# DLRM tower on one Trainium2 core: six fields picked on TensorE instead of four, 13 gathers a block, smaller rings

## What is computed

```
e = stack([tbl_f[ids[:, f]] for f in range(32)], axis=1)      # [2048, 32, 256]
dots = einsum('bnd,bmd->bnm', e, e)
z = dots[:, iu, ju]                                           # i < j, 496 numbers
h = concatenate([z, dense_ctx], axis=1)                       # 496 + 16 = 512
h = maximum(h @ W_top1 + b_top1, 0)                           # 512 -> 512
h = maximum(h @ W_top2 + b_top2, 0)                           # 512 -> 256
y = h @ W_top3                                                # 256 -> 1
```

## Time and profile before

| | |
|---|---|
| median of 3 runs | 613.19 us (612.56 to 613.61) |
| the profiled execution: its time | 611.16 us |
| the profiled execution: its span | 609.4 us, 25960 instructions |
| PE busy | 522.0 us, 86% |
| POOL busy | 432.3 us, 71% |
| DVE and ACT busy | 275.0 us (45%) and 218.9 us (36%) |
| moved by DMA | 72.16 MB, mean 118 GB/s |
| granted TensorE clock, mean | 0.992 of 2.4 GHz |

### The profile page before, as it was taken

One profiled execution on the slowest core, in us unless ns is written; L12 is line 12 of the kernel. 1 busy time (PEld: TensorE's weight loads), 2 busy tenths in 40 slices (PEclk: granted clock), 3 DMA queues, 4 the chain that ended last, 5 costly groups with the idle time before them and its releaser, 6 DMA issues.

```text
span 609.4 us, 25960 instructions
## 1 busy us (share of the span) xinstructions
PE 522.0 (86%) x11962; PEld 463.2 (76%) x11962; DVE 275.0 (45%) x596; ACT 218.9 (36%) x423; POOL 432.3 (71%) x463
## 2 busy tenths in 40 slices
PE   1349998999999998899889897988889798899875
PEld 0235795988888897879879796977879697887654
DVE  2003844737274645556354455546254555415231
ACT  1233334343333333334323334433323433343540
POOL 6776677777777777777777777777777777777700
PEclk9999999999999999999989999999999999999997
DMA  5587543443434343434334343433434333333300
GB/s 145 192 238 228 141 135 109 113 122 107 123 110 127 109 122 108 124 111 118 115 107 124 109 126 108 121 111 108 126 108 123 107 109 110 109 107 107 107 12 3
DMA packets 26415, 72.16 MB, mean 118 GB/s; under 512 B 8426, under 2 KB 9338, under 8 KB 25680
## 3 DMA queue, kind: packets, MB, share of 16 engines
q0 software_dynamic: 21888, 59.80, 35.6%
q1 hardware_dynamic: 4420, 10.72, 5.6%
HBM read 70.48 MB, written 0.01 MB: 116 GB/s over the span
## 4 chain that ended last, share of the span: by engine, by line
PE 65%; POOL 13%; DMA 10%; issue 9%; DVE 1%; ACT 1%; SPq 0%
PE ps_l L324 15%; PE ps_turn L240 15%; POOL rows L227 13%; PE ps_gram L291 12%; DMA rows<-in_table,index 10%; PE ps_pick L269 7%; PE ps_pick L271 7%; PE ps_l L338 2%; PE ps_l L255 1%; PE ps_pick L255 1%; PE ps_l L346 1%; DVE pairs L592 1%; PE ps_turn L355 0%; PE ps_wide L355 0%; PE ps_l L355 0%
## 5 line engine op out<-in xcount | busy, mean ns | idle before, releaser
L227 POOL DMA_INDIRECT rows<-in_table,index x456 | 431.5, 946 | 145.2 <-issue 120.9
L456 ACT COPY cols<-ps_turn 128x512 f32<-128x512 f32 x221 | 128.3, 590 | 320.2 <-PE ps_turn L240 319.9
L592 DVE COPY pairs<-ps_gram 32x112 f32<-32x112 f32 (+1 forms) x480 | 180.6, 376 | 134.5 <-PE ps_gram L291 128.4
L240 PE MATMUL ps_turn<-identity,rows 128*128 128x128 f32 x912 | 147.8, 290 | 51.1 <-DMA rows<-in_table,index 50.8
L240 PEld LDWEIGHTS ps_turn<-identity,rows 128*128 128x128 f32 x912 | 103.0, 145 | 69.7 <-DMA rows<-in_table,index 47.9
L291 PE MATMUL ps_gram<-cols 128*32 128x32 f32 x7936 | 108.9, 200 | 20.9 <-issue 19.4
L291 PEld LDWEIGHTS ps_gram<-cols 128*32 128x32 f32 x7936 | 90.1, 110 | 46.3 <-issue 41.4
L580 DVE TENSOR_TENSOR one_hot<-ps_wide,row_number 125x2048 fp32r<-125x2048 f32 x28 | 63.9, 2282 | 116.0 <-ACT ps_wide L473 115.9
L269 PE MATMUL ps_pick<-one_hot,table_hi 125*128 125x256 f32 x448 | 114.8, 294 | 0.4 <-ACT stage L477 0.4
L324 PE MATMUL ps_l<-pairs,w_sb 128*128 128x128 f32 x960 | 109.9, 275 | 0.6 <-DVE score L611 0.6
L271 PE MATMUL ps_pick<-one_hot,table_lo 125*128 125x256 f32 x448 | 110.0, 283 | 0.0
(11 more groups left out here) (63 smaller groups left out, 140.0 us busy)
## 6 DMA issues: line engine op xcount, KB each, us to landing
rows<-in_table,index POOLq DMA_INDIRECT x456
pick_id<-in_pick_ids SPq DMA_DIRECT2D x14, 250.0 KB
w_sb<-in_w_t SPq DMA_DIRECT2D x1, 2048.0 KB, 23.1
cols<-in_tbl SPq DMA_DIRECT2D x2, 1000.0 KB
stage<-in_tbl SPq DMA_DIRECT2D x2, 1000.0 KB
w_sb<-in_W_top SPq DMA_DIRECT2D x1, 512.0 KB, 26.8
pairs<-in_dense_t SPq DMA_DIRECT2D x16, 8.0 KB, 2.1
scores<-score SPq DMA_DIRECT2D x16, 0.5 KB
```

The source lines that it names most:

```text
L227: pool.indirect_dma_start(out=rows[x % ROWS][:, k, :], out_offset=None, in_=table, in_offset=bass.IndirectOffsetOnAxis(ap=index[:, t, i:i ...
L240: last = pe.transpose(ps_turn[x % TURNS][:, h, SPG * k:SPG * (k + 1), :], rows[x % ROWS][:, k, h * P:(h + 1) * P], identity[:, :])
L456: act.copy(cols[t % COLS][:, :, :, FPU * u:FPU * (u + 1)], ps_turn[x % TURNS][:, :, :, :]).then_inc(cols_ready, 1)
L592: last = dve.tensor_copy(pairs[n % 2][N_FIELDS * q:N_FIELDS * (q + 1), c0:KC, TQ * j + FQ * u:TQ * j + FQ * (u + 1)] .rearrange("p c g -> ...
```

## The change

- `PICKS` is 6: two more fields of 1000 rows are picked. 26 fields are left to gather in blocks 4 to 31: six whole units (`WHOLE`) of two gathers and a seventh with one gather, 2 fields of 64 samples. A block has 13 gathers, the kernel 64 + 28 * 13 = 428. There are 42 jobs; from block 5 on each tile period has three, one in the odd block (u = 4, 5) and two in the even (u = 1, 2 and u = 4, 5), up to block 28.
- The ring `rows` has 6 units in place of 8, `cols` 2 blocks in place of 3. `raw` is gone, and the DMA descriptor scratch of a partition is set to 4096 bytes.
- `split_table` is gone from PE. ACT makes the high part as before, DVE subtracts it from the table (`make_lo`). The raw tables land in `w1_sb` and `stage`, so that the weights of layer 1 are loaded after three tables are split.
- `relu2` and `take_score` go from DVE to ACT. Gram of an odd block (done in the even one) starts at u = 0, gram of an even block is in two pieces in place of four; layer 2 is at u = 3 and layer 3 at u = 6 of an even block. In the last block `early_layer1` of the first half stands behind the last transposes.

```
-PICKS = 4
+PICKS = 6
-    ROWS, COLS, TURNS = 8, 3, 3
+    ROWS, COLS, TURNS = 6, 2, 3
+    def jobs(t):
+        if 2 <= t < SETTLED:                      # SETTLED = 5
+            return [2 * t - 4, 2 * t - 3]
+        q = 3 * ((t - SETTLED) // 2) + PICKS
+        return [] if t < 2 or q >= JOBS else [q] if t % 2 == 1 else [q + 1, q + 2]
-        return {2: (0, 4), 3: (4, 8), 4: (8, 12), 5: (12, 16)} if t % 2 == 1 else {1: (0, 6), 2: (6, 11), 3: (11, 16)}
+        return {2: (0, 8), 3: (8, 16)} if t % 2 == 1 else {0: (0, 6), 1: (6, 11), 3: (11, 16)}
...
-            sp.wait_ge(table_loaded[0], 16)
-            load_table(2)
-            sp.wait_ge(table_loaded[1], 16)
+            for j in range(2, 4):
+                sp.wait_ge(table_loaded[j - 2], 16)
+                load_table(j)
+            sp.wait_ge(lo_ready, 3)
+            load_table(4)
             sp.dma_start(w1_sb[:, :, :], w1_t).then_inc(w1_loaded, 16)
...
+                    if t >= 1 and u in gram_parts(t):
+                        gram(t - 1, *gram_parts(t)[u])
+                    if 3 <= t < BLOCKS - 1 and t % 2 == 1:
+                        if u == 1:
+                            layer1((t - 3) // 2)
+                    if 4 <= t and t % 2 == 0:
+                        if u == (0 if t == BLOCKS - 2 else 3):
+                            layer2((t - 4) // 2)
+                        if u == (2 if t == BLOCKS - 2 else 6):
+                            layer3((t - 4) // 2)
+                    if t % 2 == 0 and jobs(t):
+                        if u in (1, 2):
+                            pick(jobs(t)[0], u - 1)
+                        if u in (4, 5):
+                            pick(jobs(t)[1], u - 4)
+                    if t % 2 == 1 and jobs(t):
+                        if u in (4, 5):
+                            pick(jobs(t)[-1], u - 4)
...
                         if u == 5:
-                            early_layer1(0, M1C // 2)
+                            spin(1)
+            early_layer1(0, M1C // 2)
             half_gram(1)
...
# ACT, odd block with jobs: c is its job
+                        if u == 5:
+                            take_pick(c)
                     if t > BPG and t % BPG != 0 and u == (2 if t == BLOCKS - 1 else 5):
                         place(t)
...
# DVE
+            def make_lo(j):
+                dve.wait_ge(hi_ready, j + 1)
+                dve.tensor_tensor(table_lo[:, j, :, :], table_raw[j], table_hi[:, j, :, :].bitcast(F32),
+                                  ALU.subtract).then_inc(lo_ready, 1)
```

More of the change, by code:

```diff
@@ L61, in dlrm_tower, with gathers, landed @@
     LATE = N_FIELDS - EARLY
-    def last_gathers(v):
-        return [((2 * v + k) // UNITS, (2 * v + k) % UNITS) for k in range(SUBS)]
+    def gathers(t, u):
+        if t < BPG:
+            return [(s, u) for s in range(SUBS)]
+        if t < BLOCKS - 1:
+            return [(s, u) for s in range(SUBS)] if u < WHOLE else [(0, WHOLE)]
+        if u == UNITS // 2:
+            return [(0, WHOLE)]
+        v = u if u < UNITS // 2 else u - 1
+        return [((2 * v + k) // WHOLE, (2 * v + k) % WHOLE) for k in range(SUBS)]
+    def landed(x):
+        return 16 * sum(len(gathers(t, u)) for t in range(BLOCKS) for u in range(units(t))
+                        if unit(t, u) <= x and unit(t, u) % ROWS == x % ROWS)
+    def jobs(t):
[3 more added lines that the diff above has]
+        return [] if t < 2 or q >= JOBS else [q] if t % 2 == 1 else [q + 1, q + 2]
     def gram_parts(t):
@@ L233, in _, with transposes @@
         def _(pe):
-            def transposes(x):
-                pe.wait_ge(gathered[x % ROWS], 16 * SUBS * (x // ROWS + 1))
+            def transposes(t, u):
+                x = unit(t, u)
+                pe.wait_ge(gathered[x % ROWS], landed(x))
                 if x >= TURNS:
@@ L522, in regroup_half_upper, with relu2, take_score @@
                 moved.then_inc(half_pairs_ready, 1)
-            act.wait_ge(identity_ready, 1)
-            act.mul(minus_identity[:, :], identity[:, :], -1.0).then_inc(minus_ready, 1)
+            def relu2(n):
+                act.wait_ge(l2_done, n + 1)
+                for m in range(M2C):
+                    last = act.activation(hidden2[:, m, :], ps_late_l2[m] if n == TILES - 2 else ps_l1[:, m, :],
+                                          ACT.Relu, bias=b2_sb[:, m:m + 1])
+                last.then_inc(hidden2_ready, 1)
+            def take_score(n):
+                act.wait_ge(l3_done, n + 1)
+                if n >= 2:
+                    act.wait_ge(stored[n % 2], 16 * (n // 2))
+                act.copy(score[:, n % 2, :], ps_late_l3 if n == TILES - 2 else ps_l1[0:1, M2C, :]
+                         ).then_inc(score_ready, 1)
             spread_ids(0)
@@ L707 @@
     starts = np.cumsum([0] + [tables[f].shape[0] for f in order])[:-1].astype(np.uint32)
-    index_t = ids[:, order].reshape(blocks, BLOCK // SPG, SPG, units, FPU).transpose(2, 4, 0, 3, 1)
-    index_t = dram("index_t", index_t.reshape(P, -1).astype(np.uint32))
-    base_t = dram("base_t", np.repeat(np.tile(starts.reshape(units, FPU).T, (SPG, 1)), BLOCK // SPG, axis=1))
+    whole = ids[:, order].reshape(blocks, BLOCK // SPG, SPG, units, FPU).transpose(2, 4, 0, 3, 1).reshape(P, blocks, -1)
+    base_t = np.repeat(np.tile(starts.reshape(units, FPU).T, (SPG, 1)), BLOCK // SPG, axis=1)
+    rest = (N_FIELDS - PICKS) % FPU
+    n_whole = (N_FIELDS - PICKS) // FPU
+    late = order[FPU * n_whole:FPU * n_whole + rest]
+    column = BLOCK // SPG * n_whole
+    first = GROUP // BLOCK
+    index_t = whole.astype(np.uint32)
+    index_t[:, first:, column:] = 0
+    index_t[:, first:, column] = ids[:, late].reshape(blocks, P).T[:, first:]
+    base_t = np.stack([base_t, base_t], axis=1)
+    base_t[:, 1, column] = np.tile(starts[FPU * n_whole:FPU * n_whole + rest], BLOCK)
+    index_t = dram("index_t", index_t.reshape(P, -1))
+    base_t = dram("base_t", base_t)
     table = dram("table", np.concatenate([tables[f] for f in order]))
```

222 lines of the change are left out of this document (101 added, 121 removed).

## The result

The kernel after takes 677.49 us, the median of four runs (671.94 to 680.96), where the kernel before took 613.4: 1.1028 times as long, interval 1.0944 to 1.1113. The forecast was 637 us with a range of 612 to 652. The sign was right; the time lies 25 us above the upper end.

A forecast was written before the change was run, and what follows sets the result against it. POOL set the pace before (35.0 us a period, PE 32.4); PE was to become the bound at 36.8. Start 120 + 12 * 36.8 + end 71.9 = 633.5 us of span, 637 us as measured, 3.9% slower; range 612 to 652.

The forecast's parts named there:

- What bounds the kernel: Blocks 5 to 28: PE becomes the bound, 35.9 us a period with data ready against POOL's 32.5.
- The third pick, 4.1 us a period: PE, each tile period: a third pick adds two half picks of 2.07 us, 4.14 us.
- the 34.6 that was named as a sign: Tile periods: PE busy about 34.6 us in each, as a sign that the forecast holds.
- The wait for ACT, 1.35 us: Before an odd block's gram: PE waits 1.35 us a period for `place` and a copy, queued on ACT behind `take_pick`.
- The wait of layer 1: Layer 1 waits for `take_score` on ACT: 0.6 us in every second period, 0.3 us on average.
- The step that failed is gram: Gram on PE: five pieces instead of seven save 0.2 us a period, instructions ready after a wait 0.7 us of stalls.
- The third rival: PE's stalls come from the old order: 34.5 us a period without the ACT wait, 601 us; chance 0.12.
- The start: Before the tile periods: first layer 1 at about 75 us instead of 82.3, weights landing at 71 to 77 us.
- The second rival: Late weights and landings, short ring, larger gram pieces: first layer 1 at 85 us, periods of 37.6, 658 us; chance 0.12.
- the small descriptor scratch: POOL's gathers: 4096 bytes cost nothing, or at worst a slower POOL, hidden up to 1.41 us a gather.
- From the first to the second layer 1: Start, between the first two layer 1 steps: 44 to 45 us, second at 120 us (bounds 114 and 125).
- The end: From layer 1 of block 29 on: 71.9 us instead of 76.4 (bounds 69 and 75), first step 22.5 instead of 25.5.

The follow-up runs named there:

- Fourteen gathers: The kernel after, but POOL gathers the seventh unit of blocks 4 to 31 twice, 14 gathers a block: 680.04 us, 1.1115 of the kernel before.
- a shorter third pick: The kernel after, but odd blocks' job from block 5 on does only its first and last chunks (results not right): 648.32 us, 1.0574 of the kernel before.
- the mended order: The kernel after with odd blocks' gram at u = 1, 2, 3, even blocks' gram in four pieces, and `place` at u = 4: 630.83 us, 1.0262.
- the one piece: The kernel with all three orders undone (630.83 us), but gram of an even block in one piece of 128 matmuls at u = 2: 653.29 us, 1.0674.
- gram at u = 1: The kernel after, but gram of an odd block starts at u = 1 of the next block (pieces at u = 1, 2, 3): 663.34 us, 1.0818.
- with four pieces: Even blocks' gram in four pieces against two, both with odd blocks' gram at u = 1, 2, 3 and `place` at u = 4: 630.83 against 637.29 us.
- the first gap filled: The kernel after with six identity matmuls ahead of each odd block's gram from 5 to 27, where PE waits for ACT: 681.87 us, 1.1108.
- three groups of seven: All three orders undone, six picks only in groups 2, 4 and 6, four picks in the others: 606.83 us, 0.9899 of the kernel before.

## Why the prediction was right in its sign and wrong in its size

**What bounds the kernel: right.** PE took over from POOL. Fourteen gathers show no change, a shorter third pick takes off 2.9 us a period.

**The third pick, 4.1 us a period: right.** Three picks fill 12.0 us of a period on the timeline of after, 4.0 each. PE's busy time, 35.1 us a period at full clock, is 0.5 above the 34.6 that was named as a sign.

**The wait for ACT, 1.35 us: right in place and size** (17.1 us in the twelve periods, 1.43 each). The wait of layer 1 was forecast at 0.6 us in every second period; up to 600 us it is 3.4 us in 6, 0.57 each. The seventh, 2.2 us, lies in the end.

**The step that failed is gram.** The text took 0.2 us off for five pieces instead of seven, and then "a gram that starts after a wait should find its instructions ready; I take off 0.7 us of the 1.4 us of stalls". Both have the wrong sign. Of the 28.0 us of stalls 20.9 lie in the twelve periods: 1.7 us a period and not 0.7. In nine of the twelve a stall follows in the very gram that waited for ACT, 11.8 us in all (one is shown below, at 422.78), so a gram that starts after a wait doesn't find its instructions. The other 9.1 us lie in the gram of two pieces. And the dense runs themselves go slower: 2.06 us for 128 where two pieces of 64 take 1.5 to 2.0 in the mended order; PE's busy time is 0.5 us a period above the 34.55 of the mended kernel's clean periods. Together 1.5 us of the 1.84 by which the clean periods lie above the forecast (38.64 - 36.8; 22 us in twelve); 0.1 more is the wait for ACT, the rest small gaps. The cause is shown by the packets of instructions, by the one piece (+25 us) and by the edits that lay longer work between the pieces: the stalls fell by 12.6 us with gram at u = 1, and from 15.6 to 5.7 us with four pieces. The third rival said that the stalls belong to the order of the work, not to PE, and gave 34.5 us a period. The mended order came to 34.88 at best. So it was right that the order makes the stalls, and wrong on which order: it blamed the four pieces, and expected the new order to be the better one.

**The clock was no term of the sum.** Three periods at 0.96 took 2.3 us more each, 7 us; of the 2.3 us PE's busy time is 1.4 and the rest is longer gaps. The kernel before has one such period too, at 0.95. A stretch ahead of a fall, then the window behind it, with its granted clock of 0.66:

```profile
418.68 1.26 PE L298 MATMUL ps_gram<-cols 128*32 128x32 f32 x96 [1.43 <-ACT cols L463]
419.87 0.66 PE L263 MATMUL ps_turn<-identity,rows 128*128 128x128 f32 x4
420.46 0.38 PE L298 MATMUL ps_gram<-cols 128*32 128x32 f32 x19
422.78 0.79 PE L298 MATMUL ps_gram<-cols 128*32 128x32 f32 x61 [1.94 <-issue]
423.50 0.58 PE L276 MATMUL ps_pick<-one_hot,table_hi 125*128 125x256 f32 x1
423.88 0.42 PE L278 MATMUL ps_pick<-one_hot,table_lo 125*128 125x256 f32 x1
```

```profile
424.50:428.00 3.50, 3.50 (x23) 3.50 (x22) 0.00 (x0) 0.36 (x1) 0.12 (x1) 0.66 0.07 22
```

PE had stood 1.43 us for ACT and 1.94 us for instructions within 5.5 us, and then the picks of 256 columns follow each other every 0.21 us and not 0.12: the lower level, 1.2 GHz. What lets it fall isn't settled: with the first gap filled one period still fell, and in the period from 127.92 on PE stood for 1.42 and 1.43 us within 5.3 us and the clock stayed at 1.00.

**The start: 8 us late.** The first layer 1 was put at 75 us and began at 83.3. The step that failed is what layer 1 waits for. The sum had it wait for the gathers of unit 25 and for its weights. It waited for neither: PE's last wait for a gather ends at 63.74 us, and the 19.6 us from there to layer 1 are nearly all PE's own work, four half picks among it, with one stall of 2.21 us and a first half pick at the lower clock, 3.5 us where the next took 2.0. Before 63.74 PE was behind on landings: it was busy for 9.64 of the 27 us from 42 to 69, and the gather issued at 52.23 landed 11.46 us later, within the 4 to 12 that were named. The second rival came close to the number (85 us). Of its reasons, the late landings held PE up until 63.74 only, and the weights didn't hold it up.

The text also put the small descriptor scratch at nothing. The timeline of POOL in the start says otherwise:

```profile
37.54 2.74 POOL L249 DMA_INDIRECT rows<-in_table,index  x1 [0.30 <-issue]
40.59 2.13 POOL L249 DMA_INDIRECT rows<-in_table,index  x1 [0.30 <-issue]
```

The same happens at 45.52 (2.65 us) and 55.99 (2.47 us), and twice between 85 and 110 us. A gather else takes 0.95. In each of the fifteen runs with 4096 bytes six gathers take 1.9 to 3.0 us, all ahead of 112 us, 8 to 10 us in all. In the two runs without it, the kernel before and the same with a ring of 6, none takes over 1.3 us, although DMA was as busy in the start (254 GB/s from 33 to 42 us). That points to the scratch, but no run changes it alone. Three of the long gathers lie ahead of the one issued at 52.23, so they may have cost the start up to 4.7 us.

From the first to the second layer 1 it was 44.6 us, 44 to 45 forecast.

**The end: 7 us late.** The last stretch of 48.1 us is 1.3 us shorter than forecast. The stretch before it was put at 22.5 us by POOL's last gather and took 30.3:

```profile
611.28 0.34 PE L298 MATMUL ps_gram<-cols 128*32 128x32 f32 x17 [1.12 <-issue]
611.55 2.05 PE L263 MATMUL ps_turn<-identity,rows 128*128 128x128 f32 x14
614.38 1.56 PE L298 MATMUL ps_gram<-cols 128*32 128x32 f32 x94 [0.78 <-ACT cols L463]
617.43 0.47 PE L298 MATMUL ps_gram<-cols 128*32 128x32 f32 x34 [1.49 <-issue]
617.84 3.64 PE L344 MATMUL ps_l<-hidden,w_sb 128*128 128x128 f32 x16
...
628.73 1.02 PE L331 MATMUL ps_l<-pairs,w_sb 128*128 128x128 f32 x7 [2.19 <-ACT score L548]
```

Gram stalls here too, layer 2 runs at half clock, and layer 1 waits 2.19 us for the score, which is on ACT now. In the mended order the stretch takes 26.5 us at clock 1.00, so some 4 us are order and clock. The other 4 are a misreading: POOL wasn't the bound there any more. PE needs its own 22.2 us of work, the wait of 2.2 us for the score (it stays in the mended order) and some gaps. No run took this stretch alone.

**The sum of the misses:** 7.8 + 28.9 + 6.6 = 43.3 us of span, 633.5 + 43.3 = 676.8.

**Adding up the change itself:** of 64 us lost, 47 are the order in which the new pieces were put, and come back when three steps are moved. The other 17 are the trade itself, with the smaller rings, the scratch and the late tables that it brought; no run takes these apart. By the span of the mended kernel (631.0 us, second layer 1 at 127.88, first stretch of the end from 553.71 on) the twelve periods take 35.5 us each where they took 34.3, 14.2 us in all, the start 6.5 us more, the end 0.9. That makes 21.6 us between these two profiled executions; the 17 are from the ratios. Made only in three groups of seven, the trade comes out 1% ahead of the kernel before.

**Not tried:** the descriptor scratch alone; the new kernel with four picks everywhere; two column blocks alone, since the raw tables lie in the third; and eight units in the ring of after, since there is no room for them.

## What to carry to other kernels

When two engines need nearly the same time, don't move work over as a whole: move it in every second stretch, so that both need the mean. A new order of queues needs its own sum, for each reader of each queued step, and short matmuls should be laid in pieces with longer ones between them, never in one dense run, and not with only a few transposes between. Before an idea is judged by its time, put its order right: here the order cost nearly three times what the idea did.

## What the runs showed of the hardware

- Matmuls of 32 columns outrun the supply of instructions. The stalls of gram end 2.2 to 3.0 us after the start of a packet of 16384 bytes on the instruction queue (70 stalls in four runs), and a run of 128 such matmuls uses up as many instructions in 2.06 us. Pieces of 64 took 0.76 to 0.99 us, and a run of 256 was cut by a stall of 1.69 us; in all 5.7 us of stalls with short pieces and half picks between, 19.4 with short pieces and transposes between (the kernel before), 25.4 with that gram in one. The Trainium skill, "Runtime: NRT & Kernel Launch", section "Instruction fetch mechanics", says that instructions come in blocks of 256 and that crossing a block is mostly hidden; the traces agree with the first and disagree with the second for such runs.
- In the start DMA moved 227 GB/s from 42 to 69 us, and the gather issued at 52.23 landed 11.46 us later. POOL did not keep its pace of 1.25 us there: four gathers between 37 and 59 us took 2.1 to 2.7 us each and not 0.95.
- With descriptor scratch of 4096 bytes all fifteen runs have such long gathers, six each, and the two runs without it have none; behind 112 us POOL keeps its pace, also with fourteen gathers a block. The Trainium skill, "SBUF — State Buffer", section "SBUF size: 192, 224, or 256?", names 16 KiB for this ring. That a quarter of it makes the long gathers is likely but not tested by itself.
- At a granted clock of 0.55 over 27 us PE was busy for 9.64 us only; what that level cost there isn't shown. The half pick that came behind it at the lower level took 3.5 us and the next 2.0. A tile period with a granted clock of 0.96 had 1.4 us more of busy time on PE and took 2.3 us longer.
